# Router with its own weights standing, and row statistics inside the attention stream: one core of Trainium2

## What is computed

```python
x = x + tanh(g_xattn[1]) * xattn1(layernorm(x), ctx, ...)      # causal attention, 16 heads of 32
x = x + tanh(g_ffn[1]) * moe(layernorm(x), Wr, br, gate_bias, ...)

def moe(x):                                  # 1600 rows of 512
    gate = x @ Wr + br                       # Wr: 512 x 7
    _, ids = top_k(gate + gate_bias, 2)
    probs = softmax(gate where chosen, else -inf)
    u = x @ Wup[e] + bup[e]
    g = silu(u @ Wgate[e] + bgate[e]) * u
    out = sum_e probs[e] * (g @ Wdown[e] + bdown[e])
    return out + the same for one shared expert, for every row
```

## Time and profile before

| | us |
|---|---|
| median of 3 runs (lowest, highest) | 2217.43 (2213.9, 2219.85) |
| the profiled execution, its own time | 2218.61 |
| span in its profile | 2216.9 |
| causal attention, from its first work to the barrier | 1409.4 to 1648.5 |
| expert stage, from its first work to its first block's transposes | 1649.4 to 1706.0 |
| PE, DVE, ACT, POOL busy over the span | 1946.2, 1421.1, 959.1, 509.1 |

### The profile page before, as it was taken

One profiled execution on the slowest core, in us unless ns is written; L12 is line 12 of the kernel. 1 busy time (PEld: TensorE's weight loads), 2 busy tenths in 40 slices (PEclk: granted clock), 3 DMA queues, 4 the chain that ended last, 5 costly groups with the idle time before them and its releaser, 6 DMA issues. The chain is left out here.

```text
span 2216.9 us, 33553 instructions
## 1 busy us (share of the span) xinstructions
PE 1946.2 (88%) x11866; PEld 1541.6 (70%) x11866; DVE 1421.1 (64%) x2759; ACT 959.1 (43%) x1983; POOL 509.1 (23%) x469
## 2 busy tenths in 40 slices
PE   1899999999499999999913999799959989999997
PEld 1677787777377777877711555466639879999996
DVE  3666666676666666666767777366664544666663
ACT  1333344443233333344465333355524425666663
POOL 3211010110311110001022000133220354565553
PEclk9999999999699999999956999899985999999999
DMA  5200000000321001000051000000013147777774
GB/s 135 74 6 33 37 37 37 37 1 1 76 74 38 2 35 37 37 37 1 1 227 63 0 0 0 1 1 1 1 61 98 40 126 166 236 237 232 230 238 99
DMA packets 39530, 154.61 MB, mean 70 GB/s; under 512 B 5472, under 2 KB 12848, under 8 KB 29050
## 3 DMA queue, kind: packets, MB, share of 16 engines
q1 hardware_dynamic: 27170, 128.39, 16.5%
q0 software_dynamic: 11408, 23.37, 5.8%
q10 hardware_dynamic: 840, 1.36, 0.2%
HBM read 132.59 MB, written 20.51 MB: 69 GB/s over the span
## 5 line engine op out<-in xcount | busy, mean ns | idle before, releaser
L608 DVE TENSOR_TENSOR la_q_roped<-banks,la_rope_q 128x400 f32<-128x400 f32 x384 | 197.9, 567 | 45.6 <-PE banks L400 28.6
L555 ACT ACTIVATE la_probs<-banks,la_minus_max 100x361 f32<-100x361 f32 x256 | 145.0, 566 | 157.2 <-DVE la_minus_max L643 157.2
L643 DVE TENSOR_REDUCE la_minus_max<-banks 100x1 f32<-100x361 f32 x256 | 135.7, 530 | 58.9 <-PE banks L426 52.1
L1751 DVE TENSOR_TENSOR ex_weights_low<-ex_raw_weights,ex_weights_high 128x2048 fp32r<-128x2048 f32 x60 | 137.4, 2290 | 51.2 <-ACT ex_weights_high L1658 48.5
L343 POOL TENSOR_TENSOR la_wq_high<-la_weights,zero 128x1024 fp32r<-128x1024 f32 x14 | 26.5, 1894 | 609.6 <-PE banks L372 609.6
L435 PEld LDWEIGHTS banks<-identity,la_probs 100*121 100x121 f32 x768 | 113.4, 184 | 64.3 <-DVE la_probs L650 29.6
L446 PE MATMUL banks<-la_probs_t,la_kv_rows 121*128 121x200 f32 x768 | 151.3, 333 | 0.0
L925 PE MATMUL banks<-qf_sign_weights,qf_x_quant_t 128*100 128x512 bf16 x512 | 122.9, 391 | 32.2 <-DVE qf_hidden L1006 18.1
L573 ACT COPY la_probs_t<-banks 121x300 f32<-121x300 f32 x256 | 106.2, 415 | 96.3 <-PE banks L435 96.3
L2007 POOL TENSOR_TENSOR ex_g_low<-ex_g,ex_g_high 128x256 fp32r<-128x256 f32 (+1 forms) x104 | 86.7, 949 | 232.6 <-ACT ex_g_high L1690 232.1
L435 PE MATMUL banks<-identity,la_probs 100*121 100x100 f32 x768 | 125.6, 272 | 16.0 <-DVE la_probs L650 14.5
(11 more groups left out here) (312 smaller groups left out, 5501.6 us busy)
## 6 DMA issues: line engine op xcount, KB each, us to landing
ex_raw_weights<-w_exp SPq DMA_DIRECT2D x60, 1024.0 KB
la_weights<-w_pack SPq DMA_DIRECT2D x16, 1984.0 KB, 7.8
qf_raw_weights<-w_ffn SPq DMA_DIRECT2D x2, 4096.0 KB
qf_raw_weights<-w_ffn SPq DMA_DIRECT2D x2, 2048.0 KB
out<-ex_block_out POOLq DMA_DIRECT2D x13, 256.0 KB, 4.4
residual<-x SPq DMA_DIRECT2D x1, 3200.0 KB
normed_rows<-ex_xn SPq DMA_DIRECT2D x16, 200.0 KB
out<-residual SPq DMA_DIRECT2D x4, 800.0 KB
```

What stands on the lines that cost most here:

```text
L555: act.activation(prob[:, s % 4, 0:L], ps[0:S, s % 2, 0:L], ACT.Exp, bias=nmax[:, s % 4:s % 4 + 1], accum_out=sums[:, s % 4:s % 4 + 1]).the ...
L608: dve.tensor_tensor(roped[:, h, v, c, :].rearrange("p (b s) -> p b s", b=GB), ps[:, B_BANKS[k % 2], 0:NT].rearrange("p (b s) -> p b s", b=GB),
L643: dve.tensor_reduce(nmax[:, s % 4:s % 4 + 1], ps[0:S, s % 2, 0:L], AX.X, ALU.max, negate=True).then_inc(s_max, 1)
L1751: dve.tensor_tensor(wl[:, m, :], raw[:, m, :], wh[:, m, :].bitcast(F32), ALU.subtract).then_inc(w_low[m], 1)
```

## The change

Two things, in the last two stages.

**Statistics.** The 16 `bn_stats` at the start of the expert stage go. In the attention loop VectorE takes them one by one, at the end of slots s = 11, 15, ... 71 (`STATS_AT` = 11), for sequence (s - 11) / 4, behind `low`, and the loop gets two more slots, in which nothing else is done.

**Router.** The router's weights are no longer split and now stand (8 columns), while x^T moves, in float32, for four sequences (400 columns) at a time: 4 matmuls for each of 4 groups. The transposed rows are copied out of PSUM unsplit, by ScalarE for even t and VectorE for odd t (`turned`). The result, logits^T (8 x 400), is copied by ScalarE (`logits`) and turned back by 16 small transposes (`turn_logits`). The buffers for x^T and logits^T lie on tiles that are free at that time (`block_out`, `g`). Rows are normalised by GpSimd (even t) and ScalarE (odd t) into 6 buffers instead of 4, with a semaphore each. The splits of the shared expert's matrices move to t = 4, 8, 12 (ScalarE) and 7, 11, 15 (VectorE). The wait for the small loads moves behind the copies on VectorE, and stands ahead of the first transpose on TensorE.

```diff
@@ causal_attention
+        STATS_AT = OUT_AT + 2
+        SLOTS = ITEMS + STATS_AT - KC + 1
...
+                    if s >= STATS_AT and (s - STATS_AT) % KC == 0:
+                        b = (s - STATS_AT) // KC
+                        dve.wait_ge(o_add, b + 1)
+                        dve.bn_stats(core.stats[:, b, :], core.x[:, b, :]).then_inc(n_bn, 1)
@@ expert_ffn, SyncE
-                    sp.wait_ge(normed, t + 1)
-                    sp.dma_start(rows[t * S:(t + 1) * S, :], xn[:, t % 4, :]).then_inc(rows_out[t % 4], 16)
+                    sp.wait_ge(normed[t % 2], t // 2 + 1)
+                    sp.dma_start(rows[t * S:(t + 1) * S, :], xn[:, t % XR, :]).then_inc(rows_out[t % XR], 16)
@@ ScalarE
-                row_norm(0)
                 row_norm(1)
-                for t in range(B):
-                    if t + 2 < B:
-                        row_norm(t + 2)
-                    act.wait_ge(x_t, t + 1)
-                    if t >= 2:
-                        act.wait_ge(x_free, t - 1)
-                    act.copy(xth[:, t % 2], ps[:, t % 2, 0:KC * S].rearrange("p (k s) -> p k s", k=KC)).then_inc(x_high, 1)
-                    if t in (4, 7, 10):
-                        high(0, (t - 4) // 3)
+                row_norm(3)
+                for t in range(0, B, 2):
+                    if t + 5 < B:
+                        row_norm(t + 5)
+                    turned(t)
+                    if t % GB == 2 and t > GB:
+                        logits(t // GB - 1)
+                    if t in (4, 8, 12):
+                        high(0, t // 4 - 1)
+                logits(GROUPS - 1)
@@ VectorE
-                norm_stats_dve(dve, core, ns, range(B))
+                for t in range(B):
+                    dve.bn_aggr(core.mv[:, t, :], core.stats[:, t, :]).then_inc(ns.var, 1)
+                norm_rstd_dve(dve, core, ns.std, ns.rstd, range(B))
+                for t in range(1, B, 2):
+                    turned(t)
+                    if t in (7, 11, 15):
+                        low(0, t // 4 - 1)
@@ GpSimd
+                pool.wait_ge(ns.rstd, 6)
+                for t in range(0, B, 2):
+                    if t >= XR:
+                        pool.wait_ge(rows_out[t % XR], 16 * (t // XR))
+                        pool.wait_ge(x_t, t - XR + 1)
+                    pool.tensor_scalar(xn[:, t % XR, :], core.x[:, t, :], core.rstd[:, t:t + 1],
+                                       core.nmr[:, t:t + 1], ALU.mult, ALU.add).then_inc(normed[0], 1)
@@ TensorE
+                def route(g):
+                    for k in range(2):
+                        pe.wait_ge(x_out[k], 2 * (g + 1))
+                    if g >= 2:
+                        pe.wait_ge(lt_out, g - 1)
+                    for k in range(KC):
+                        mm = pe.matmul(ps[0:EA, 4 + g % 2, 0:NT], wr[:, k, :], xt[:, g % 2, k, :],
+                                       start=(k == 0), stop=(k == KC - 1))
+                    mm.then_inc(x_routed, 1)
...
+                pe.wait_ge(small_in, 128)
+                for t in range(B):
+                    turn_x(t)
+                    if t % GB == 1 and t > GB:
+                        route(t // GB - 1)
+                route(GROUPS - 1)
+                for g in range(GROUPS):
+                    turn_logits(g)
                 turn(0)
                 up(0)
```

More of the change, by code:

```diff
@@ L1447 @@
 PGW = 64 + EA
+XR = 6
 def tiles_of(j):
@@ L1493, in expert_ffn @@
         zero = sb("zero_rows", [128, D])
+        yflat, gflat = y[:].rearrange("p i d -> p (i d)"), gm[:].rearrange("p k n -> p (k n)")
+        XT = 2 * KC * NT
+        xt = yflat[:, 0:XT].rearrange("p (g k n) -> p g k n", g=2, k=KC)
+        lt = [a.rearrange("p (g n) -> p g n", g=2) for a in (yflat[0:EA, XT:XT + 2 * NT], gflat[0:EA, 0:2 * NT])]
         bias, bsel = sb("biases", [128, EA, 2 * KC]), sb("block_biases", [128, RB + 1, 2 * KC])
@@ L1596, in rows_of @@
                     last = min(B - 1, (BN * j + BT * n - 1) // S)
-                    for k in range(4):
-                        sp.wait_ge(rows_out[k], 16 * len(range(k, last + 1, 4)))
+                    for k in range(min(XR, last + 1)):
+                        sp.wait_ge(rows_out[k], 16 * len(range(k, last + 1, XR)))
                     if BN * j + BT * n > N_TOK:
@@ L1660, in row_norm, with turned, logits @@
                 def row_norm(t):
[L1661 to L1665, removed]
+                    if t >= XR:
+                        act.wait_ge(rows_out[t % XR], 16 * (t // XR))
+                        act.wait_ge(x_t, t - XR + 1)
+                    act.activation(xn[:, t % XR, :], core.x[:, t, :], ACT.Identity, bias=core.nmr[:, t:t + 1],
+                                   scale=core.rstd[:, t:t + 1]).then_inc(normed[1], 1)
+                def turned(t):
+                    g = t // GB
+                    act.wait_ge(x_t, t + 1)
+                    if g >= 2:
+                        act.wait_ge(x_routed, g - 1)
+                    act.copy(xt[:, g % 2, :, t % GB * S:(t % GB + 1) * S],
+                             ps[:, t % 4, 0:KC * S].rearrange("p (k s) -> p k s", k=KC)).then_inc(x_out[0], 1)
+                def logits(g):
+                    act.wait_ge(x_routed, g + 1)
+                    act.copy(lt[g // 2][:, g % 2, :], ps[0:EA, 4 + g % 2, 0:NT]).then_inc(lt_out, 1)
                 def block_high(j):
@@ L2112, in down_bias, with turn_x, turn_logits @@
                     pe.matmul(ps[0:S, 2 + t % 2, :], pgt[:, t, :], bdr[:], start=True, stop=True).then_inc(b_psum, 1)
-                def route(t):
-                    pe.wait_ge(x_low, t + 1)
+                def turn_x(t):
+                    pe.wait_ge(normed[t % 2], t // 2 + 1)
+                    if t >= 4:
+                        pe.wait_ge(x_out[t % 2], (t - 4) // 2 + 1)
                     for k in range(KC):
-                        for i, (a, m) in enumerate(((xth, wrh), (xth, wrl), (xtl, wrh))):
-                            mm = pe.matmul(ps[0:S, 4, t * EA:(t + 1) * EA], a[:, t % 2, k, :], m[:, k, :],
-                                           start=(k == 0 and i == 0), stop=(k == KC - 1 and i == 2))
-                    mm.then_inc(x_free, 1)
+                        mm = pe.transpose(ps[:, t % 4, k * S:(k + 1) * S], xn[:, t % XR, k * 128:(k + 1) * 128],
+                                          core.ident[0:S, 0:S])
+                    mm.then_inc(x_t, 1)
+                def route(g):
+                    for k in range(2):
+                        pe.wait_ge(x_out[k], 2 * (g + 1))
+                    if g >= 2:
+                        pe.wait_ge(lt_out, g - 1)
[3 more added lines that the diff above has]
+                    mm.then_inc(x_routed, 1)
+                def turn_logits(g):
+                    pe.wait_ge(lt_out, g + 1)
+                    for i in range(GB):
+                        t = g * GB + i
+                        mm = pe.transpose(ps[0:S, 6, t * EA:(t + 1) * EA], lt[g // 2][:, g % 2, i * S:(i + 1) * S],
+                                          core.ident[0:EA, 0:EA])
+                    if g == GROUPS - 1:
+                        mm.then_inc(lg_done, 1)
                 def rank():
```

48 lines of the change are left out of this document (16 added, 32 removed).

## The result

The changed kernel takes 2203.84 us (median of 5 runs, 2198.97 to 2206.72); the kernel before took 2217.43 beside it (2213.03 to 2219.85). The ratio is 0.9944, its 95% interval 0.9926 to 0.9963: faster by 0.56%. The profiled execution of after took 2198.97 us, its span is 2197.3, against 2218.61 and 2216.9 of before.

What follows compares the result with a forecast made beforehand. Bounds: VectorE's statistics, then TensorE's router chain, in the expert stage's opening; VectorE and TensorE alternating in the attention loop. Routing -20.5 plus statistics +5.4 gives -15.1 us from 2218.61: 2203 us, 8-in-10 range 2196 to 2211.

Steps and rivals of the forecast that it cites:

- The statistics no longer opening the stage: Expert stage's opening: first row normalised 3.0 us after first work, 9.3 us earlier than before, nearly all of it eaten afterwards.
- The queue as the next limit: Expert stage's opening: row writes wait behind 3 MB of matrices, ScalarE idles about 10 us, first route at about 1667.5.
- Rival (b): Expert stage's opening: rows land sooner, the queue is no wall, ScalarE flows; 23.6 us net saved, 2195 us; chance 0.12.
- row 9 lands in time: DMA queue in the opening: row 9, which row 15 needs, lands at about 1674, in time.
- Two passes for a float32 matmul: Routing on TensorE: a 400-column float32 matmul costs twice a split one, so a route takes 3.04 us at 1.2 GHz.
- Rival (d): Routing: float32 matmuls need four passes, a route takes 5.4 us at the lower level; 2.3 us net saved, 2216; chance 0.02.
- The level: TensorE's clock in the routing: rises from 1.2 to 2.4 GHz after a route or two; routing ends at 1685.5.
- rival (a): Routing stays at 1.2 GHz throughout and ends at 1688.7; 11.9 us saved with the statistics, 2207 us; chance 0.26.
- The statistics in the loop: Attention loop: statistics of 0.60 us each on VectorE cost 5.4 us in all, bounds 1 and 9.6.
- the eight named slots: Attention loop: less_max of slots 16, 20, 32, 36, 48, 52, 56, 60 later by 0.6 us each, 4.8 in all.
- the five named ones: Attention loop: statistics of slots 11, 23, 27, 39, 43 are followed by a q slot and cost nothing.
- rival (c): Attention loop loses its clock from slot 48 on, costing up to 19.5 us; slower than before, 2223 us; chance 0.04.

Runs made afterwards that it cites:

- Experiment 1: The changed kernel with the 16 row statistics back at the start of the expert stage and none in the attention loop: 2197.87 us, ratio 0.9922.
- experiment 6: The changed kernel with x^T and router rounded to fp32r, one pass, low parts left out: 2202.21 us in one execution.
- experiment 2: The kernel before, old router kept, with only the statistics moved into the attention loop: 2220.36 us, ratio 1.0023.
- experiment 3: The changed kernel with the loads of the shared expert's three matrices issued behind rows 0 to 5 instead of ahead: 2208.17 us, ratio 0.9971.
- experiments 10 to 12: The changed kernel with statistics ahead of the additions, plus eight row buffers, matrix loads between rows, or both: 2192.81, 2193.11 and 2190.49 us.

## Why the prediction was right or wrong

**The time.** 2203 forecast, 2203.84 measured. The agreement is closer than the steps deserve: two terms were off by 2 us each, both making it slower, and the rest of the kernel, not in the sum, was 3.4 us shorter in the profiles.

**The statistics no longer opening the stage: right.** The first norm is 2.98 us after the first work, by the prediction 3.0. Experiment 1 confirms the other half: nearly all of the 9.3 us is eaten, 0.7 is left.

**The queue as the next limit: right**, in place and in size. ScalarE was to stand about 10 us ahead of its fourth norm and stood 11.13; the first route was to start 18.1 us after the first work and started at 18.55. Rival (b) falls. The step "row 9 lands in time" held only just: ScalarE waited 0.33 us for it, to 1680.25, some 4 us later in the stage than the prediction had it, since rows don't move at the matrices' rate (last section). TensorE's wait for the small loads (it turned the first row at 1656.19 and not at about 1655.2) lay inside the long wait and cost nothing.

**Two passes for a float32 matmul: wrong.** This is the step that failed, and a sign of being wrong that the prediction had named came: the first route took over 3.5 us. The prediction read the earlier trace rows's "x4 3.04" as four matmuls. They are two: a k piece is one matmul, there are 16 in the stage, and that line's group in before's trace (records; ns of the shortest, middle and longest; first and last start) has 32 records:

```profile
L1215 PE MATMUL banks<-ca_latents_t,ca_weights x32: 497/525/1036, 1417.6 to 1567.6; 128*128 128x400 f32 x32
```

The route takes 5.50 us at 1.2 GHz and 2.85 at 2.4, not 3.04 and 1.5. Rival (d), given 0.02, had the right mechanism, and the rule in the Trainium skill, page "FP8 and Floating Point Precision", section "TensorE Precision Notes", that true float32 makes four passes, was right against my reading; experiment 6 agrees, with 0.67 us for each of a matmul's two records against 0.33 for the one. The same was in the earlier trace rows, where a split matmul took 0.34. The rival's time, 2216, didn't come, because it took the lower level throughout. In the forecast's own case (the clock up behind the first route) the error is 2.5 us for the first route and three times 1.35 for the others, 6.5 us. Most of this was covered by accident. With an early rise TensorE's own work from the first route on would have been some 13.1 us by the prediction's figures (3.0 and three times 1.5 for the routes, 4.0 for transposes, about 0.5 for a copy, 1.1 at the end); ScalarE was to bind at 15.6, and the forecast took 18.0, the middle between the levels. Measured were 19.7, near the sum of 13.1 and 6.5, and the chain behind the first route lies on TensorE but for one copy: TensorE bound it, not ScalarE. So the opening ended 2 us late, 38.3 and not 36.1, and saved 18.2 instead of 20.5, inside the bounds of 17 to 23.

**The level: right, by luck in part.** The rise after a route or two came, after the first. It hangs on what was mis-read, as far as one execution shows: with the short routes of experiment 6 it didn't come at all, which is what rival (a) described. Those are half as long as the two-pass routes that the prediction had in mind, so what those would have done isn't shown.

**The statistics in the loop: the pattern right, the size wrong.** Exactly the eight named slots kept a delay and the five named ones gave it back. The delays sum to 4.2 us and not 4.8, three of them being 0.40: there the maximum had started 0.75 us after the start of `low` and not 0.55, so that 0.2 us of the delay was absorbed; of that, 0.11 us was idle time, too little to be listed. The tail was 0.7 (0.6 forecast). The rest, 3.2 us, is rival (c)'s mechanism in small: two projections of 1.6 us each at the lower level. That price is the one the prediction read from the earlier trace rows; it was left out of the sum as an ordinary case. The prediction's "and no others" so failed for slots 50 and 54. Term 5.4, measured 7.4.

**Behind block 0: not foreseen in full.** The turn of block 0 is at the higher level and gives 0.8 us, as said. The other 2.6 us of the shorter rest also appear in experiment 2 (508.5 us), which has the old router, so the router isn't their cause. The rest took 507.5 to 509.6 us in the profiles of the change and its variants, whose code there is the same, and of the kernel before there is one profile (510.9); so most of it may be a difference between executions. The cause stays open.

## What to carry over

Check the count of a group's records against the matmuls in the code before taking a mean from it; one float32 matmul is two records here. When a wait for a queue is to be removed, add up what the queue must carry before the end of the stretch: another order of the same bytes moves the wait (experiment 3), and more buffers or an order in between shorten the opening by 3 to 4 us of 38.7 (experiments 10 to 12). Put small extra work on an engine into the slot where it waits anyway; on this kernel that alone was worth 6 us by the ratios (the loop was 7.3 us shorter), about half as much as the change itself gained.

## What the hardware showed that I had not expected

Writes of 100-row tiles don't use the whole DMA capacity. Stretches of after:

```profile
1656.00:1664.00 8.00, 4.26 (x24) 3.95 (x24) 1.72 (x3) 1.17 (x2) 0.79 (x2) 0.50 0.98 357
1678.00:1684.00 6.00, 5.97 (x31) 2.42 (x28) 4.82 (x5) 5.67 (x7) 3.85 (x8) 1.00 0.57 211
```

While the 128-row matrices load, the engines are 98% busy and move 357 GB/s; in the second stretch rows are written, with a fetch of a block of rows beside them up to 1679.4 and little left behind 1683, at 57% and 211 GB/s; from 1680 to 1682, where only rows are written, it is 63% and 236. At that rate a row of 200 KB takes 0.9 us and not the 0.6 of the prediction, and sixteen take some 14. The Trainium skill, page "DMA: Bandwidth & Descriptors", section "Why a DMA increments its semaphore by 16 and not by 1", says that a DMA runs on the largest number of engines up to 16 that divides its outer dimension, 10 for 100 partitions; the trace agrees, 63% being 10 of 16.

More work on TensorE can cost less than it weighs. With four passes instead of one the four routes took 8 us more (14.05 against 5.99), but block 0 came only 1.8 us later (38.3 against 36.5). TensorE had stood for 3.4 us between the short routes, waiting for ScalarE, and 0.7 between the long ones; and behind the first long route it went to 2.4 GHz, where ten sequences' transposes took 4.2 us instead of 7.6.
